# One tile shape of the matrix array for every matmul of a filtered leaky ReLU: 64 rows by 128 columns instead of 128 by 64 in the down-sampling

## The reference

```
lin     = einsum('oc,chw->ohw', W, coord) + b        # 512 channels, 256x256 coordinates
x       = x + sin(lin)                               # x is [2, 512, 256, 256], float32
x       = x + bias[channel]
x       = fir12(x, up_filter * 2, up=2)              # along w, then along h: 512x512
x       = leaky_relu(x, 0.2) * sqrt(2)
out     = fir12(x, down_filter, down=2)              # along w, then along h: 256x256
```

## Time and profile before

| | |
|---|---|
| median of 3 runs | 6572.86 us (6572.68 to 6572.97) |
| the profiled execution | 6572.63 us |
| its span, first to last instruction | 6570.9 us |
| granted TensorE clock over the span | 1.000 |
| PE busy, PEld busy | 6509.3 us (99%), 6210.1 us (95%) |
| DVE, ACT, POOL busy | 4002.7, 3980.8, 1303.7 us |
| DMA engines busy | 27.2% |

### The profile page before, as it was taken

How to read it: one execution, slowest core, us unless ns; L and a number is a source line. 1 busy time by engine, 2 the same in 40 slices (tenths; PEclk the granted TensorE clock), 3 DMA queues, 4 the chain that set the end, 5 groups by cost and what they waited for, 6 DMA issues and landing times.

```text
span 6570.9 us, 361569 instructions
## 1 busy us (share of the span) xinstructions
PE 6509.3 (99%) x148480; PEld 6210.1 (95%) x148480; DVE 4002.7 (61%) x6218; ACT 3980.8 (61%) x7688; POOL 1303.7 (20%) x1041
## 2 busy tenths in 40 slices
PE   6999999999999999999999999999999999999999
PEld 6999999999999999999999999999999999999999
DVE  6666666666666666666666666666666666666665
ACT  4666666666666666666666666666666666666665
POOL 2111111111111111111111111111111111111111
PEclk9999999999999999999999999999999999999999
DMA  3222222222222222222222222222222222222222
GB/s 121 85 84 84 85 85 85 84 84 83 83 84 85 85 85 85 85 85 83 85 85 85 85 83 83 83 84 85 85 85 85 85 85 83 84 85 85 85 84 78
DMA packets 580065, 558.27 MB, mean 85 GB/s; under 512 B 40400, under 2 KB 574928, under 8 KB 580048
## 3 DMA queue, kind: packets, MB, share of 16 engines
q1 hardware_dynamic: 580048, 558.02, 27.2%
HBM read 278.94 MB, written 278.92 MB: 85 GB/s over the span
## 4 chain that ended last, share of the span: by engine, by line
PE 99%; DVE 1%; DMA 0%; SPq 0%; issue 0%; ACT 0%; DVEq 0%; POOL 0%; POOLq 0%
PE p_ps L433 34%; PE y_ps L449 32%; PE o_ps L433 15%; PE a_ps L449 14%; PE o_ps L459 3%; DVE up_band L377 0%; DVE angle L354 0%; DVE angle L352 0%; DVE phase L344 0%; ACT trig L258 0%; DVE trig_parts L361 0%; DVE angle L356 0%; DVE turns L348 0%; DVE turns L350 0%; DVE trig_parts L360 0%
## 5 line engine op out<-in xcount | busy, mean ns | idle before, releaser
L392 DVE SCALAR_TENSOR_TENSOR z<-y_ps,leak 128x512 f32<-128x512 f32 x4096 | 2629.3, 684 | 1749.8 <-ACT leak L278 1749.8
L278 ACT ACTIVATE leak<-y_ps 128x512 f32<-128x512 f32 x4096 | 2280.0, 623 | 2108.0 <-PE y_ps L449 2107.6
L449 PE MATMUL y_ps<-up_band,a_sb 64*128 64x138 f32 (+2 forms) x32768 | 2539.2, 282 | 1.4 <-ACT a_sb L271 1.3
L433 PE MATMUL p_ps<-down_band,z 128*64 128x68 f32 (+1 forms) x65536 | 2440.8, 227 | 1.7 <-DVE p_rows L400 1.7
L245 POOL TENSOR_TENSOR x_sum<-x_raw,f_sb 128x512 f32<-128x512 f32 x1024 | 1291.3, 1283 | 5235.6 <-ACT f_sb L264 5226.3
L433 PEld LDWEIGHTS p_ps<-down_band,z 128*64 128x64 f32 x65536 | 2156.2, 137 | 160.6 <-DVE z L392 1.0
L449 PEld LDWEIGHTS y_ps<-up_band,a_sb 64*128 64x128 f32 x32768 | 2163.4, 186 | 75.1 <-issue 1.5
L400 DVE COPY p_rows<-p_ps 128x512 f32<-128x512 f32 x2048 | 1416.2, 691 | 802.3 <-PE p_ps L433 699.1
L449 PE MATMUL a_ps<-up_band,x_sum 64*128 64x138 f32 (+2 forms) x16384 | 1306.6, 275 | 28.6 <-POOL x_sum L245 28.5
L433 PE MATMUL o_ps<-down_band,p_rows 128*64 128x68 f32 (+1 forms) x32768 | 1170.2, 224 | 0.8 <-DVE p_rows L400 0.8
L449 PEld LDWEIGHTS a_ps<-up_band,x_sum 64*128 64x128 f32 x16384 | 1132.9, 187 | 29.4 <-POOL x_sum L245 29.0
(11 more groups left out here) (28 smaller groups left out, 43.0 us busy)
## 6 DMA issues: line engine op xcount, KB each, us to landing
x_raw<-in_x_dram SPq DMA_DIRECT2D x1024, 256.0 KB, 3.1
out_dram<-o_out SPq DMA_DIRECT2D x1024, 256.0 KB, 2.5
f_rows<-trig_dram SPq DMA_DIRECT2D x512, 20.0 KB
trig_dram<-trig_parts SPq DMA_DIRECT2D x32, 256.0 KB, 2.5
trig_dram<-ones SPq DMA_DIRECT2D x4, 256.0 KB, 2.4
trig_dram<-bias_wide SPq DMA_DIRECT2D x4, 256.0 KB, 2.5
up_taps<-in_L_conv_up_filter_dram SPq DMA_DIRECT2D x1, 6.0 KB, 2.3
down_taps<-_L_conv_down_filter_dram SPq DMA_DIRECT2D x1, 6.0 KB, 2.4
```

The lines of the kernel that those rows point to most:

```text
L278: nc.scalar.mul(leak[i % 2][:, :], y_ps[i][:, :], SLOPE * GAIN).then_inc(leak_done, 1)
L392: nc.vector.scalar_tensor_tensor(z[n][:, i, :], y_ps[i][:, :], GAIN, leak[i % 2][:, :], ALU.mult, ALU.max).then_inc(z_done, 1)
L433: last = nc.tensor.matmul(out_ps[half * HALF:(half + 1) * HALF, lo:hi], data[:, t, col:col + HALF], down_band[:, band:band + hi - lo], sta ...
L449: last = nc.tensor.matmul(outs[o][:, lo:hi], data[row, k, (at + o) * P:(at + o + 1) * P], up_band[row, band:band + hi - lo], start=step == ...
```

## The change

All matmuls use the array as 2 tiles of 64 rows by 128 columns. `step_of` replaces `up` and `down`. For the down stages the 512 rows of an operand are cut in 8 blocks of 64 rows, each of which reaches 36 or 40 output columns. `down_rows` and `down_cols` get half steps like the up stages, with the semaphores `p_half` and `o_half`. `p_ps` becomes two banks, and both are full before they are copied: one by ACT (`copy_p0`), one by DVE (`copy_p1`). `down_cols` writes its result into the two banks `a_ps`; `sines` writes into the first two banks `y_ps`. `copy_a` is split between ACT and DVE, and `copy_f` moves from ACT to DVE, where it stands between `leaky` 1 and `leaky` 2 of the slots with n = 1. `f_rows` has 3 rows, in plain float32, at partitions 0 and 64, the other rows zeroed; the tables have 3 rows instead of 10 and are saved in 4 DMAs for each 128 channels instead of 10.

```diff
-    DN_SPAN = [(0, 68, 4), (60, 132, 0), (124, 196, 0), (188, 256, 0)]
+    DN_SPAN = [[(max(0, 32 * g - 4), min(H, 32 * g + 36), max(0, 32 * g - 4) + 4 - 64 * (g // 2)) for g in (2 * k, 2 * k + 1)]
+               for k in range(UT)]
+    DOWN_COLS = 128
+    P_PLACE = (0, 2, 1, 3)
...
-        p_ps = pb("p_ps", [P, 2, H])
-        o_ps = pb("o_ps", [P, HT, WID])
+        p_ps = [pb(f"p_ps{o}", [P, 2, H]) for o in range(2)]
...
+            def step_of(cols, outs, data, band, spans, at, where, ks, step, fresh=True):
+                pe.sem_inc(steps_begun, 1)
+                for k in ks:
+                    for rows in range(2):
+                        o = rows ^ step
+                        row = slice(rows * HALF, (rows + 1) * HALF)
+                        lo, hi, start = spans[k][rows]
+                        for part in range(0, P, cols):
+                            col = (at + o) * P + part
+                            last = nc.tensor.matmul(outs[o][part:part + cols, lo:hi], data[row, where[k], col:col + cols],
+                                                    band[row, start:start + hi - lo], ...)
...
+            def slot(c, n, ...):          # TensorE
+                m = 2 * c + n
+                up_cols(m, n, 0, 0, c + 2 if n == 0 and f_before else None, ...)   # n == 0: waits f_copied >= c + 2
+                up_cols(m, n, 1, 0)                                                # waits z_done >= 4 * m
+                up_rows(m + 1, 1 - n, 0, first)
+                up_cols(m, n, 0, 1)
+                up_rows(m + 1, 1 - n, 1)
+                up_cols(m, n, 1, 1)
+                down_rows(m - 1, 1 - n, 0, 0)
+                down_rows(m - 1, 1 - n, 0, 1)
+                down_cols(m - 2, n, 0, m + 2 if a_next else None)
+                down_rows(m - 1, 1 - n, 1, 0)
+                down_cols(m - 2, n, 1)
+                if f_next and n == 1:
+                    sines(c + 2, 4 * m + 2)                                        # waits z_done >= 4 * m + 2
+                down_rows(m - 1, 1 - n, 1, 1)
...
+            def slot(c, n, ...):          # VectorE
+                copy_a1(m + 1, 1 - n)
+                leaky(m, n, 0)
+                leaky(m, n, 1)
+                if f_next and n == 1:
+                    copy_f(c + 2)                                                  # waits f_made >= c + 3
+                leaky(m, n, 2)
+                leaky(m, n, 3)
+                copy_p1(m - 1, 1 - n)
...
+            def slot(c, n, ...):          # ScalarE
+                leaky(m, 0)
+                copy_a0(m + 1, 1 - n)
+                leaky(m, 1)
+                leaky(m, 2)
+                leaky(m, 3)
+                copy_o(m - 2, n, 16 * (c - 1))
+                copy_p0(m - 1, 1 - n)
```

More of the change, by code:

```diff
@@ L412, in slot @@
                 if p:
-                    copy_p(m - 1, 1 - n, 1)
+                    copy_p1(m - 1, 1 - n)
+            copy_f(0)
+            copy_a1(0, 0)
+            copy_f(1)
             slot(0, 0, p=False)
             slot(0, 1)
-            slot(1, 0)
-            slot(1, 1)
-            with dve.Fori(2, C) as c:
+            with dve.Fori(1, C - 2) as c:
                 slot(c, 0)
                 slot(c, 1)
-            slot(C, 0, y=False)
+            slot(C - 2, 0)
+            slot(C - 2, 1, f_next=False)
+            slot(C - 1, 0)
+            slot(C - 1, 1, a_next=False, f_next=False)
+            slot(C, 0, a_next=False, y=False)
         @block.tensor
         def _(pe):
[L426 to L437, removed]
-            def up(data, outs, at, step):
-                for k in range(HT):
+            def step_of(cols, outs, data, band, spans, at, where, ks, step, fresh=True):
+                pe.sem_inc(steps_begun, 1)
+                for k in ks:
                     for rows in range(2):
@@ L458, in sines @@
+                return last
+            def sines(c, z_from):
+                pe.wait_ge(f_rows_loaded, 32 * c + 32)
+                reached(pe, z_done, z_from)
+                pe.sem_inc(steps_begun, 1)
                 for t in range(HT):
-                    last = nc.tensor.matmul(o_ps[:, t, :], f_rows[:, t * P:(t + 1) * P], f_rows[:, H:H + WID],
-                                            start=True, stop=True)
+                    row = slice(t * HALF, (t + 1) * HALF)
+                    for part in range(0, P, DOWN_COLS):
+                        col = t * P + part
+                        last = nc.tensor.matmul(y_ps[t][part:part + DOWN_COLS, 0:WID],
+                                                f_rows[row, col:col + DOWN_COLS], f_rows[row, H:H + WID],
+                                                start=True, stop=True, skip_group_check=True)
@@ L499, in slot, with down_rows @@
[L499 removed]
+                    step_of(P, outs, a_sb[n], up_band, UP_SPAN, 2 * pair, range(HT), range(HT), 1).then_inc(y_made, 2)
+            def down_rows(m, n, step, pair):
+                if step == 0:
+                    if pair == 0:
+                        pe.wait_ge(z_done, 4 * m + 4)
+                        reached(pe, p0_copied, m)
+                        reached(pe, p1_copied, m)
+                elif pair == 0:
+                    pe.wait_ge(p_half, m + 1)
+                last = step_of(DOWN_COLS, [p_ps[o][:, pair, :] for o in range(2)], z[n], down_band, DN_SPAN, 2 * pair,
+                               range(UT), range(UT), step, pair == 0)
+                if pair == 1:
+                    last.then_inc(p_made if step else p_half, 1)
```

263 lines of the change are left out of this document (128 added, 135 removed).

## The result

The changed kernel takes 10562.29 us (median of 4 runs, 10560.53 to 10564.01), against 6572.91 us before: the ratio is 1.6069, with a 95% interval of 1.6041 to 1.6097. The direction was forecast, the size was not: 9090 us, with 8600 to 9460 us as the range. Some 1470 us are missing from the sum.

What follows compares the result with a forecast made beforehand. PE was taken to bound the kernel: 2 x (2.77 up + 5.28 down) + 0.43 sines + 1.1 waits = 17.63 us a channel, 9027 us for 512, plus 59 us setup, fill and drain; forecast 9090 us, range 8,600 to 9,460 us.

Steps and rivals of the forecast that it cites:

- What bounds the kernel: PE, busy 99% of the span, sets the time: 12.70 us a channel before, at a granted clock of 1.00.
- A down pair goes from 0.0606 to 0.110 us, load-bound: Down stages: two tiles' matmuls become paced by loading 128 columns; 48 pairs add 2.37 us a slot.
- The joints: Extra time where down and up stages turn into each other and at a `copy_p` wait; goes, -0.42 us a slot.
- The counter: `steps_begun` adds one sequencer instruction a step, 12 a slot; taken to cost nothing.
- The waits of `copy_f`: Next slot's `up_cols` waits for f (0.28 us) and z (0.83 us late): together 1.1 us a channel.
- The setup: Shorter sine-table work and fewer saves take 10 us off the 69 us of setup, fill and drain.
- The up stages: They keep shape and widths: 24 pairs at 0.1155 us, 2.77 us a slot.
- Rivals 4 and 5: Each step's first load exposed: 10,420 us, chance 5%; load and stream not overlapping: 10,660 us, chance 3%.

Runs made afterwards that it cites:

- run with 72 columns: Changed kernel with down spans widened from 36 or 40 to 68 or 72 columns, the added ones meeting zeros: 9215.93 us.
- 64-column tiles: Changed kernel with tiles of 64 rows by 64 columns in down stages and sines: 11294.8 us; with TensorE's loop body cut to one channel, 7140.76 us.
- run of before with 40 columns: Kernel before the change with down spans cut to 40 columns, leaving out part of the filter's sum: 6445.51 us.
- With 72 columns and without waits: Changed kernel with down spans of 68 or 72 columns, `copy_f` behind `leaky` 3 and sines ahead of `down_cols`' second half step: 8631.71 us.
- run without waits: Changed kernel, down spans still 36 or 40 columns, with `copy_f` behind `leaky` 3 and sines ahead of `down_cols`' second half step: 10939.56 us.
- that with 20 columns: Kernel before the change with down spans cut to 20 columns, leaving out part of the filter's sum: 6638.07 us.

## Why the prediction was wrong

Point by point, with the terms of its sum:

- **What bounds the kernel**: right. PE before, PE after.
- **A down pair goes from 0.0606 to 0.110 us, load-bound**: right; 0.111 us. The run with 72 columns, which keeps the pair at 0.111 us, and that with 64-column tiles, which halves it, show that the load of the 128 columns is what takes the time. The run of before with 40 columns adds that a load-bound pair takes 0.003 to 0.005 us more than the bare load.
- **The joints go, -0.42 us a slot**: right at the full clock. With 72 columns and without waits, up follows down at 0.98 us for 16 matmuls where it was 0.66 + 0.46 for 16.
- **The counter costs nothing**: right.
- **The waits of `copy_f`, 1.1 us a channel**: right at the full clock, 1.14 us. Of the two parts, f was taken too low (0.28 us, measured 0.42) and z too high (0.83 us, measured 0.73), and that the total came so near is in part luck. DVE's work of a channel adds up to 9.0 us and not 9.1, which changes nothing.
- **The setup, 10 us shorter**: not borne out. With the full clock (72 columns) a channel takes 17.86 us, from the sines at 88.98 us to those at 9160.08 us, 508 channels later. That leaves 71 us of the span of 9214 us for setup, fill and drain, where the sum had 59 and the kernel before has 69. The second sines came at 55.96 us in the changed kernel instead of 62.51, 6.5 us sooner and not 12; where the rest went was not taken apart. All terms together were 128 us or 1.4% short: 12 in the setup and 116 in the channels. The pair of 0.1113 us (0.89 / 8) instead of 0.110 makes some 60 of these and the waits some 20.
- **The failed step** is the tacit one in "What bounds the kernel now" and "The up stages": the granted clock of 1.00, read from rows of before, was carried over to the changed kernel, and the up stages were costed as if nothing ahead of them mattered. The prediction had itself worked out that a down pair would stream for 0.034 of 0.110 us, where it streams for nearly all of 0.061 before, and took the thin stream for a saving. The clock fell to 1.2 GHz behind the down stages for a third of the time, which costs the difference of the two runs with and without it: 10559.0 - 9214.1 = 1345 us of span, 2.6 us a channel. With that, 9086 + 128 + 1345 = 10559 us, which adds up by construction, since the last two terms are measured differences. As a cross-check, a third of a channel of 20.48 us is 6.8 us, and at half the clock that would cost 3.4 us if PE worked all the time; the wait for z, 0.73 us at the full clock, falls into it and is nearly hidden, which leaves an estimate of 2.7 us. What makes the clock fall behind one down stage and not behind another stays open, as the run without waits and that with 20 columns show.
- **The range** took the bounds of each term but had no case in which the clock moved, and so ended 1100 us too low. Rivals 4 and 5 gave about the right time for a wrong reason.

## What to carry to other kernels

A matmul with its own weights costs the longer of its load and its stream; cutting the stream below the load saves nothing and thins out the array's work. Before a time is forecast from one clock, work out for each stage how thin its streams will be, and where they get much thinner than in the present profile, add a case in which the clock halves in the stages behind it. If it does, wider streams of zeros can be worth more than fewer columns; and while the clock moves, don't judge a wait by taking it away.

## What the runs showed of the hardware

- Streaming more columns made a kernel 13% faster (10562 to 9216 us), and at another tile shape 40 columns were faster than 20 (6446 against 6638 us), both through the granted clock (0.834 to 0.999, and 1.00 against 0.963). The Trainium skill ("TensorE: Matmul & The Clock Gate", Part 1) states that the clock is gated by how busy PE has been; here PE's busy time in the profile is 98% and its loads' 97% in the changed kernel, and 96% and 94% in the run with 72 columns, whose clock is 0.999, so the busy shares of the profile don't show what lowers it.
- A weight load slows down with the granted clock as a stream does: 16 load-bound down matmuls take 0.89 us at 1.00 and 1.71 us where it is 0.52 on average.
- With standstills of PE of 1.4 to 3 us the clock was 0.864, and 0.998 with the same streams and tiles without them; idle times of 0.2 and 0.5 us a channel left it at 0.999.
- Four tiles of 64 by 64 load side by side: four instructions every 0.058 us.
- A loop body of TensorE with two thirds more loads and matmuls raised the instruction fetches from 0.23 to 37.68 MB and added standstills of up to 3 us; halving it took 4154 us off (11294.8 to 7140.8), part of which is again the clock (0.864 to 0.998).
